# Stacking keys and queries by SBUF copies, and one exponential per pair of heads over two PSUM banks

## The reference, cut to what matters

```python
# token mixer, for 32 sequences of L=256 positions, 256 channels
num = einsum('ts,nsd->ntd', exp(w_bias * mask), exp(k) * v)
den = einsum('ts,nsd->ntd', exp(w_bias * mask), exp(k))
h = (sigmoid(q) * num / den) @ out_w + out_b + x
h = layernorm(h) * ln_g + ln_b
# a class token is put before the 256 positions, then attention with 16 heads of 16
z = layernorm(h)
q, k, v = holo(z)                      # (z @ basis) @ (amp * cos(phase))
h = h + holo(softmax(q @ k.T * 0.25) @ v)
# feed-forward: a shared part and 2 of 8 experts for each token
```

## Time and profile before

| | |
|---|---|
| time, median of 3 runs | 2958.11 us (2955.83 to 2960.87) |
| the profiled execution | 2954.87 us, span 2953.0 us |
| busy of the span: TensorE, DVE, ACT, GpSimd | 88%, 61%, 38%, 21% |
| mean granted TensorE clock | 0.916 of full |
| bytes moved by DMA | 140 MB, mean 47 GB/s |

### The profile page before, as it was taken

One profiled execution on the slowest core, in us unless ns is written; L12 is line 12 of the kernel. 1 busy time (PEld: TensorE's weight loads), 2 busy tenths in 40 slices (PEclk: granted clock), 3 DMA queues, 4 the chain that ended last, 5 costly groups with the idle time before them and its releaser, 6 DMA issues. The chain is left out here.

```text
span 2953.0 us, 57443 instructions
## 1 busy us (share of the span) xinstructions
PE 2595.7 (88%) x16871; PEld 2124.6 (72%) x16872; DVE 1788.6 (61%) x4711; ACT 1124.9 (38%) x2993; POOL 626.0 (21%) x581
## 2 busy tenths in 40 slices
PE   2689999999999999999996557499999899999999
PEld 2467777777776776767763446377777699999999
DVE  6466767777667777767761787733333345555555
ACT  0135444445454454444452211044444423333332
POOL 1212212112122121121101675500000022222222
PEclk9589999999999999999996555599999999999999
DMA  2000000000000000000000443222222211122211
GB/s 75 8 8 23 20 16 20 23 16 20 17 23 20 16 20 19 20 20 16 16 9 14 160 131 116 93 82 83 84 85 84 78 54 57 57 64 62 59 57 54
DMA packets 88092, 140.13 MB, mean 47 GB/s; under 512 B 13986, under 2 KB 59860, under 8 KB 87764
## 3 DMA queue, kind: packets, MB, share of 16 engines
q1 hardware_dynamic: 74836, 101.99, 11.5%
q0 software_dynamic: 13056, 35.67, 3.7%
HBM read 83.04 MB, written 54.03 MB: 46 GB/s over the span
## 5 line engine op out<-in xcount | busy, mean ns | idle before, releaser
L735 DVE TENSOR_REDUCE mx<-ps 128x1 f32<-128x257 f32 x1024 | 394.5, 416 | 238.4 <-PE ps L385 214.6
L582 ACT ACTIVATE pT<-ps 128x257 f32<-128x257 f32 x1024 | 343.2, 382 | 285.1 <-PE ps L402 283.8
L385 PE MATMUL ps<-km,q 128*128 128x258 f32 x1024 | 351.3, 360 | 46.8 <-DVE mx L735 23.9
L402 PE MATMUL ps<-q,km 128*128 128x258 f32 x1024 | 283.6, 304 | 2.1 <-ACT pT L582 2.1
L385 PEld LDWEIGHTS ps<-km,q 128*128 128x128 f32 x1024 | 197.4, 193 | 118.5 <-DVE mx L735 57.2
L928 POOL TENSOR_TENSOR rs<-rs,mhalf 128x2 f32<-128x2 f32 x32 | 22.5, 703 | 1004.3 <-DVE rs L687 1004.3
L402 PEld LDWEIGHTS ps<-q,km 128*128 128x128 f32 x1024 | 192.5, 193 | 46.6 <-issue 28.7
L1564 PE MATMUL ps<-zhi,whi 128*128 128x256 f32 x1056 | 214.2, 284 | 1.5 <-DVE zlo L1632 1.5
L1564 PE MATMUL ps<-zhi,wlo 128*128 128x256 f32 x1056 | 211.1, 281 | 0.0
L1564 PE MATMUL ps<-zlo,whi 128*128 128x256 f32 x1056 | 210.6, 281 | 0.0
L1694 POOL TENSOR_TENSOR mark<-rowid 128x1 f32<-128x1 f32 x33 | 6.5, 197 | 860.4 <-DVE idx L1650 860.4
(11 more groups left out here) (321 smaller groups left out, 6278.8 us busy)
## 6 DMA issues: line engine op xcount, KB each, us to landing
z<-zs SPq DMA_DIRECT2D x140, 128.0 KB, 2.0
ys<-z SPq DMA_DIRECT2D x140, 128.0 KB, 1.9
hb<-hscr SPq DMA_DIRECT2D x66, 256.0 KB
xs<-in_x SPq DMA_DIRECT2D x64, 256.0 KB, 3.9
hscr<-h SPq DMA_DIRECT2D x34, 256.0 KB, 2.1
out<-acc SPq DMA_DIRECT2D x32, 256.0 KB
uu<-in_wu SPq DMA_DIRECT2D x6, 768.0 KB, 5.3
raw<-in_wu SPq DMA_DIRECT2D x6, 768.0 KB, 4.9
```

The source lines that it names most:

```text
L385: pe.matmul(ps[:, n % 2, 0:NP], q2[p % 2][:, h // 2, t * P:(t + 1) * P], km[p % 2][:, h // 2, h % 2, :], start=True, stop=True).then_inc(m ...
L402: pe.matmul(o, km[p % 2][:, h // 2, h % 2, t * P:(t + 1) * P], q2[p % 2][:, h // 2, :], start=True, stop=True).then_inc(s_ps, 1)
L582: act.activation(pT[:, n // LT, n % LT, :], ps[:, 4 + n % 2, 0:N], ACT.Exp, scale=HD ** -0.5).then_inc(s_ok, 1)
L735: dve.tensor_reduce(mx[:, t, h:h + 1], ps[:, n % 2, 0:N], AX_X, ALU.max, negate=True).then_inc(mx_ok, 1)
```

## The change

- **Stacking.** `stack`, `take_stack` and `sel` go. SP copies the 64-row halves of `qhi`, `qlo`, `khi`, `klo` inside SBUF into the stacked layout: 6 DMAs for `q2` and 12 for `km` in a step (`spread_q`, `spread_k`). The projection's columns are permuted so that each copy moves whole blocks; the rows of the maxima are now 112 and 113. `q2` gets four buffers, `qhi` and `qlo` have one.
- **Pairs over two banks.** `maxima` writes both heads of a pair to banks 0 and 1, and one `tensor_reduce` takes both; the next pair waits for it. `scores` writes a pair to banks 4 and 5, and one exponential takes both; the next pair waits for that. The points in the step where maxima (`MX_AT`) and values (`VALUES_AT`) are done are changed.
- **Class token.** The product that begins `values` becomes float32r with three stacked pieces (`vbds`, `pcs`); its pieces are made by ACT (`pce`, high part), GpSimd (`pcl`) and two DMAs. The addition of `cls_shift` moves from DVE to GpSimd (`cls_keys`).
- **Output.** `attend_out` becomes float32r with stacked pieces; DVE makes the low part (`out_low`).
- **Norms.** `mixer_norm` and `attn_norm` move from DVE to ACT (scale and bias, the bias from new small GpSimd products). `y1`, `yT`, `hn` share buffers with others.
- **Setup.** `xs` is loaded first, most of DVE's `memset`s go or move to GpSimd (`km`), and copies through SP are added for the new stacked constants.

```diff
-    VALUES_AT = (9, 12, 14)
-    MX_AT = [3, 3, 3, 2, 3, 3, 3, 2, 2, 2, 2, 2, 2, 0, 0, 0]
+    VALUES_AT = (6, 9, 12)
+    MX_AT = [2, 2, 1, 2, 2, 1, 0, 0, 0, 1, 2, 1, 2, 0, 0, 0]
...
+        def spread_q(j, p):
+
+            sp.wait_ge(lo_ok, 2 * j + 2)
+            for part, places in zip((qhi, qlo), PLACES[0]):
+                for place in places:
+                    for k in range(2):
+                        row = SLOT2 * k + HD * place
+                        sp.dma_start(q2[p % U][row:row + HD, :, :].rearrange("d (j w) l -> d j (w l)", w=FT).bitcast(F32),
+                                     part[p % 2][SLOT2 * k:SLOT2 * (k + 1), :, :].rearrange("p w l -> p (w l)").bitcast(F32)
+                                     ).then_inc(q_in, 16)
+
+        def spread_k(j, p, f):
+
+            if not isinstance(j, int) or j >= 2:
+                sp.wait_ge(s_ps, SN * (j - 2) + SN // FT * (f + 1))
+            for part, places in zip((khi, klo), PLACES[1]):
+                for place in places:
+                    for k in range(2):
+                        row = SLOT2 * k + HD * place
+                        sp.dma_start(km[p % 2][row:row + HD, k, HALF * f:HALF * (f + 1), :].rearrange("d j l -> d (j l)").bitcast(F32),
+                                     part[p % 2][SLOT2 * k:SLOT2 * (k + 1), f, :].bitcast(F32)).then_inc(k_in[f], 16)
...
+            if has(b + 1):
+                spread_k(b + 1, p + 1, 1)
+            if has(b + 2):
+                spread_q(b + 2, p + 2)
             if has(b - 1):
                 sp.wait_ge(h2_ok, b)
                 sp.dma_start(hscr[bass.ds(b - 1, 1)].rearrange("n p t d -> p (n t) d"), h2[:]).then_inc(h2_out, 16)
+            if has(b + 2):
+                spread_k(b + 2, p + 2, 0)
...
+            pe.wait_ge(mx_ok, m * MXN + i + 2)
+            for k in range(2):
+                last = pe.matmul(ps[:, k, 0:NP], q2[p % U][0:MAXROW, QAT[g], t * P:(t + 1) * P], km[p % 2][0:MAXROW, k, g, :],
+                                 start=True, stop=True)
+            last.then_inc(mx_ps, 1)
...
+            if k == 0 and (n > 0 or later(b)):
+                pe.wait_ge(s_ok, b * PAIRS + n // 2)
+            pe.matmul(ps[:, 4 + k, 0:NP], km[p % 2][0:MAXROW + 2, k, g, t * P:(t + 1) * P], q2[p % U][0:MAXROW + 2, QAT[g], :],
+                      start=True, stop=True).then_inc(s_ps, 1)
...
+            act.activation(pT[:, 2 * g:2 * g + 2, t, :], ps[:, 4:6, 0:N], ACT.Exp, scale=HD ** -0.5).then_inc(s_ok, 1)
...
         def step(b, p):
             for n in range(NH):
+                if n == 0 and has(b + 2):
+                    attn_norm(b + 2, p + 2)
                 if has(b):
-                    exps(b, 2 * n)
-                    exps(b, 2 * n + 1)
+                    exps(b, n)
...
-                        act.activation(pc[(p + 1) % 2][:], pcr[(p + 1) % 2][:], ACT.Exp, scale=HD ** -0.5).then_inc(pc_ok, 1)
+                        if has(b):
+                            act.wait_ge(pcl_ok, b + 1)
+                        act.activation(pce[:, 0:N], pcr[(p + 1) % 2][:], ACT.Exp, scale=HD ** -0.5).then_inc(pce_ok, 1)
+                        act.wait_ge(pce_ok, b + 2)
+                        act.activation(pcs[(p + 1) % 2][0:HD, :], pce[:], ACT.Copy).then_inc(pch_ok, 1)
...
+                    if n == 12:
+                        mixer_norm(b + 3, p + 3)
...
+            dve.tensor_reduce(mx[:, t, 2 * QAT[g]:2 * QAT[g] + 2], ps[:, 0:2, 0:N], AX_X, ALU.max, negate=True).then_inc(mx_ok, 1)
...
+            pool.tensor_tensor(nb2[:], mv2[:, :, 0], mneg[:], ALU.mult).then_inc(root2, 1)
+            pool.tensor_tensor(rs2[:], rs2[:], mhalf[:], ALU.pow).then_inc(root2, 1)
+            pool.wait_ge(root2, 2 * b + 2)
+            pool.tensor_tensor(nb2[:], nb2[:], rs2[:], ALU.mult).then_inc(p2, 1)
+
+        def cls_keys(m, p):
+
+            pool.wait_ge(negm_ok, m + 1)
+            pool.wait_ge(mx_ok, m * MXN + 2)
+            pool.tensor_tensor(pcr[p % 2][:], pcr[p % 2][:], negr[p % 2][0:NH, 0:N], ALU.add).then_inc(pcr_ok, 1)
+            pool.wait_ge(pch_ok, m + 1)
+            if later(m):
+                pool.wait_ge(pcs_in, 32 * m)
+            pool.tensor_tensor(pcl[:], pce[:], pcs[p % 2][0:HD, :], ALU.subtract).then_inc(pcl_ok, 1)
```

More of the change, by code:

```diff
@@ L158, in stage_a @@
     negc = sb("negc", [NH, 1])
-    vbd = sb("vbd", [NH, NH, SLOT])
+    vbds = sb("vbds", [STACKED, NH, SLOT], F32R)
+    vbd = temp(NH, SLOT)[0:NH]
+    vbh = temp(NH, SLOT)[0:NH].bitcast(F32R)
+    wo3 = temp(D)
+    wos = sb("wos", [3 * HARM, D], F32R)
     va = [sb("va%d" % p, [P, LT, NH, SLOT]) for p in range(2)]
     mx = sb("mx", [P, LT, NH])
-    pc = [sb("pc%d" % p, [NH, N]) for p in range(2)]
+    pcs = [sb("pcs%d" % p, [STACKED, NP], F32R) for p in range(2)]
+    pce = sb("pce", [NH, NP])
+    pcl = sb("pcl", [NH, NP], F32R)
     pcr = [sb("pcr%d" % p, [NH, N]) for p in range(2)]
@@ L340, in heads_qk @@
             for f in range(FT):
-                last = pe.matmul(ps[:, 2 + f, 0:N], Wz[:, n, f * P:(f + 1) * P], rT[:], start=True, stop=True)
+                last = pe.matmul(ps[:, 2 + f, 0:NP], Wz[:, n, f * P:(f + 1) * P], rT[:], start=True, stop=True)
             last.then_inc(qk_ps, 1)
@@ L348, in heads_v @@
             last.then_inc(v_ps, 1)
[L350 to L362, removed]
@@ L364, in cls_tiles @@
-        def cls_tiles(m, p):
+        def cls_tiles(m, p, n):
+            pe.wait_ge(lo_ok, 2 * m + 2)
             if later(m):
                 pe.wait_ge(negm_ok, m)
-            for n, (hi, lo) in enumerate(((khi, klo), (qhi, qlo))):
-                mm = [(x, y, f) for x, y in ((bdh, hi), (bdh, lo), (bdl, hi)) for f in range(FT)]
-                for i, (x, y, f) in enumerate(mm):
-                    last = pe.matmul(ps[:, n, 0:NP], x[:, n, f, :], y[p % 2][:, f, :], start=(i == 0),
-                                     stop=(i == len(mm) - 1))
-                last.then_inc(mx_ps, 1)
@@ new lines, in cls_tiles, with maxima @@
+            mm = [(x, y, f) for x, y in ((bdh, hi), (bdh, lo), (bdl, hi)) for f in range(FT)]
+            for i, (x, y, f) in enumerate(mm):
+                last = pe.matmul(ps[:, n, 0:NP], x[:, n, f, :], y[p % 2][:, f, :], start=(i == 0), stop=(i == len(mm) - 1))
+            last.then_inc(mx_ps, 1)
+        def maxima(m, p, i):
+            g, t = i // LT, i % LT
+            if i == 0:
+                pe.wait_ge(q_in, 16 * DMAS * (m + 1))
+                pe.wait_ge(k_in[0], 16 * DMAS * (m + 1))
+            if i == PAIRS // 2:
+                pe.wait_ge(k_in[1], 16 * DMAS * (m + 1))
+            pe.wait_ge(mx_ok, m * MXN + i + 2)
+            for k in range(2):
+                last = pe.matmul(ps[:, k, 0:NP], q2[p % U][0:MAXROW, QAT[g], t * P:(t + 1) * P], km[p % 2][0:MAXROW, k, g, :],
+                                 start=True, stop=True)
+            last.then_inc(mx_ps, 1)
@@ L546, in _ @@
         for f in range(FT):
-            last = pe.matmul(ps[96:P, 6, 0:B], basoT[:, f, :], onT[:, f, 0:B], start=(f == 0), stop=(f == FT - 1))
+            last = pe.matmul(ps[0:3 * HARM, 6, 0:B], basoT[:, f, :], onT[:, f, 0:B], start=(f == 0), stop=(f == FT - 1))
         last.then_inc(ro_ps, 1)
@@ L793, in step @@
                         ffn_stats(b - 1)
-                if has(b + 1) and n == 14:
-                    cls_shift(b + 1, p + 1)
                 if has(b + 2) and n == 2:
```

319 lines of the change are left out of this document (158 added, 161 removed).

## The result

The changed kernel takes 3134.6 us (median, 3133.0 to 3136.3) where the kernel before takes 2957.2: a ratio of 1.0598 [1.058, 1.0616]. It is slower, as I forecast, but by 177 us where I forecast 62, and outside my range.

The account below looks back on a forecast made before the run. TensorE was taken as the bound by occupancy, beside a chain of small operations in ordered queues. 2954.9 - 10 (setup) + 41 (waits) + 48 (clock) - 15 (last steps) = 3018.9, said as 3020 us, range 2985 to 3060.

Parts of the forecast that it names:

- once in half of the steps: TensorE's clock drops to 1.2 GHz after a wait in half of 29 steps, 3.3 us each: +48 us.
- My rival with the clock falling in every step: Clock falls one and a half times every step, or keys land late, or ACT reloads tables: 3119 us, chance 0.15.
- four waits of 1.6 to 2.3 us: TensorE idle within a step: 2.3 us at n=0, 2.2 at n=3, 1.6 at n=10, 1.8 at n=12.
- in every step, +96: Reading of the Trainium skill's small gaps between matmul groups: the clock would fall in every step, +96 us.
- the walk: Step timed through the engines' queues from the end of `mixer_out` at n=11: 45.2 us for 43.8, 1.5 either way.
- last three steps: Final first-stage steps, with no mixer chain: 5 us less from each, -15 us, bounds -25 and 0.
- Setup: Less buffer clearing by DVE, but new copies through SP: -10 us, first mixer matmul near 45 us instead of 55.6.
- Waits: 29 steps with a mixer behind them lengthen through queue waits: +41 us, range -2 to +85.
- TensorE's own work: Per step, from some 42 us to some 35; as the bound, 29 full steps would give back over 200 us.
- Copies through SP hidden: Stacking DMAs cost nothing, hidden by TensorE's matmuls of n=1 to 4; bounds 0 and +3 us a step.
- `mixer_norm` behind the evacuation at n=12: ACT evacuates `values` until 4.0 us before `mixer_norm`; `hn` ready at 4.8, where GpSimd started on it at 3.1 before.
- "faster" rival: The chain has slack, `mixer_q` comes at 22.5 us as before, a step takes 41.7: 2872 us, chance 0.23.

Follow-up runs that it names:

- e14: Changed kernel plus 29 fillers (short unused matmuls into bank 6) a step in TensorE's waits, nothing else touched: 3003.6 us.
- e8: Changed kernel with x loaded earlier and ACT doing `mixer_norm` ahead of the evacuation of `values` at n=12, no fillers: 3011.3 us.
- e7: Changed kernel with x loaded earlier, plus 26 fillers (unused matmuls) a step in TensorE's long waits: 2975.5 us.
- e10: e8 plus 19 fillers a step in TensorE's remaining waits: 2929.9 us, ratio 0.9911 to the kernel before.
- e12: e10 with the x load late again, as in the changed kernel: 2959.0 us.
- e13: e10 with single exponentials and reductions per head instead of pairs, and 15 fillers: 2921.2 us, ratio 0.9902 to the kernel before.
- e2: Changed kernel with DVE's small class-token copy (`clso`) moved behind the second reduction of n=3, x load still late: 3095.3 us.
- e3: Changed kernel plus 20 fillers at two places, 12 at n=3 and 8 at the end of n=15: 3096.5 us.
- e1: Changed kernel with the x load issued earlier, ahead of SP's waits for the class token's pieces: 3105.0 us.
- e15: Changed kernel plus 24 fillers a step where TensorE does not wait, 6 ahead of the scores of each of n=6 to 9: 3241.3 us.

## Why the prediction was wrong

**The step that failed is the clock.** I wrote "I let it happen once in half of the steps: 29 x 1.65 = +48; bounds nothing, and +145 for 5 us in each." It falls at least twice in every plain step, and costs 131 us (changed kernel against e14), net of the fillers' own cost; near my upper bound. My rival with the clock falling in every step (3119 us, chance 0.15) came nearest, if with one and a half falls. The error was to look for waits as long as that at the loop's turn. I counted four waits of 1.6 to 2.3 us and let the clock answer to them at a coin's toss; the trace has five, of 1.2 to 3.9 us, in a stretch where TensorE has little between them. The Trainium skill (TensorE: Matmul & The Clock Gate, A second HAM failure mode) tells of small idle gaps between groups of matmuls that make the clock swing. I had named it and its "in every step, +96"; the changed kernel's trace agrees, with two falls a step where I had priced one; e8's, where the clock held in 12 steps through waits of up to 1.6 us, shows that gaps do not always bring the fall. The second step that failed is a wait that the walk lacks, 28 us; it comes under "Waits".

**Part by part**, on the profiled executions (3133.6 against 2954.9, +178.7):

| term | forecast | measured |
|---|---|---|
| until the first `turn_maxima` | -10 | -13.8 (164.1 for 177.9) |
| 28 steps from there | +88 (waits 40, clock 48) | +182.7 (1451.2 for 1268.5): waits 64.7, clock 118.0, by e14's 1333.2 |
| last three steps | -15 | +14.4 (125.0 for 110.6) |
| behind them | 0 | -4.7 |

- Setup: right (the first mixer matmul comes at 40.1, forecast 45), but the next step gave most of it back, 59.0 us for 48.1; its clock is low for 48.8 us of it. (2.6 MB at 146 GB/s are 17.8 us, not 17.)
- Waits: too low, 40 for 64.7, and most of that for one that I missed. In e7 the same 28 steps take 1310.1 us, 41.6 more than before, with a walk that is off by 0.3 us or less up to `mixer_q` and by 0.5 at the end. But e7 has the early load. In the changed kernel comes what I missed: the late x, GpSimd's split, DVE's blocked copy, `low`. I had counted `xs` as ahead of the keys in SP's queue, and did not ask when GpSimd would then run, and beside what. The load costs 28 us with e7's clock held (e14 less e7, whose fillers differ by 3) and 29 with e10's (e12 less e10).
- TensorE's own work: from some 42 to some 35, I said; e8's clean step has 35.9.
- Copies through SP hidden: right. A `km` copy lands 2.9 us after its issue. No wait of over 1 us in the step above ends with a key or query DMA; the last of `km` is issued by +18.8 (walk 18).
- New operations: `pcr` 0.73 us (0.6), the two `z` operations together 1.08 (0.8), pairs 0.69 and 0.60 (0.68 and 0.60): near enough. ACT loads its function tables three times in either kernel, 1.28 us each, and never in a step.
- `mixer_norm` behind the evacuation at n=12: I had it in the walk, as a fact. It costs up to 1.7 us a step (e7 to e10, with 7 fillers less), 46 us in all.
- Last steps: wrong in sign. With less work beside them these steps still follow chains: 47.1, 41.6 and 36.4 us, against 43.9, 34.6 and 32.1 before. In e10 they take 44.1, 35.7 and 32.2, about as before, and in e14, with fillers but the old queues, 123.4 in all; so most of the excess seems to go with the places of the load and the norm in their queues. In e13, without pairs, they take 43.5, 33.5 and 29.1: a gain of 4.5 us at last, where I had 15. The 4.7 us behind them lie within what the second stage varies by.

**The sum from one kernel to the next**: 3134.6, less 131 for the clock (e14), less 28 for the early load (e7), less 46 for the norm's place (e10), less 9 for the pairs (e13): 2921; these steps stand on single comparisons, so each may be off by a few us. That is 36 us under the kernel before, but little of it is the work that TensorE lost. In the profiled executions (2922.5 against 2954.9, 32.4 less) 22.9 us come ahead of the first `turn_maxima`, in the setup and the warm-up steps, 11.7 from the 28 steps and 4.5 from the last three, and behind them 6.7 are lost again. So the steps give 16 us, and not the 200 of a TensorE bound. At 43.4 us a step TensorE's own work is about 36; that the chain through norms and heads is the bound there I conclude from e7 to e10, where a shorter chain made the step shorter. In the prediction's "faster" rival the chain had slack; no run showed it.

**Still open**: why the clock held in 12 of 21 plain steps of e8 and fell in the others, which have the same program and the same waits; so what a wait costs can't be foretold wait by wait. How much of e2's gain is the copy itself. What in the setup gives the 19 to 23 us, beside the earlier start of the mixer.

## What to carry to other kernels

Work taken from the engine that sets the pace is not time won: ask what chain is then the bound, and whether the gaps that open slow the engine's clock. Here 7 us less work for TensorE opened gaps that cost 131 us, and fillers into an unused bank, placed in the waits and nowhere else, brought them back; but even so the steps were hardly shorter than before. And when a transfer is moved in a queue, follow it to the engine that it releases, and look what runs on the neighbouring engine at that time.

## What the runs showed of the hardware

- In the changed kernel's step the granted clock fell behind waits of 1.28 and 2.05 us (948.00 and 952.47 above) and behind one of 3.90, in steps of e3 and e8 behind one of 1.17 or 1.18, and stayed at 1.2 GHz for 3.4 to 13.7 us in those. In other steps of e8 it held through waits of 1.17 to 1.61 us. Each us at the low clock cost 0.38 us (e8: 4.9 us for 12.9) to 0.41 us (e1: 1.4 us for 3.4).
- Once the clock falls, it lengthens the chain that caused the waits: from the first maxima of n=0 to `turn` are 5.1 us in the changed kernel's step, and 3.7 in e14's, which has the same queues.
- A DVE copy of 128x4 elements, 0.16 us alone, took up to 2.61 us beside a GpSimd instruction.
- Fillers of 128x512 cost 0.15 us each in a stretch where TensorE doesn't wait (e15).
